# The two local attention stacks as one sequence of 48 rows each, with the feed-forward in pieces between the head pairs

## The reference, cut to what matters

```python
for i in range(DEPTH):                      # DEPTH = 6
    x = attn_layer(shift_tokens(x), Wqkv[i], q_scale[i], k_scale[i], Wo[i]) + x
    x = ffn_layer(shift_tokens(x), ln_g[i], ln_b[i], W1[i], b1[i], W2[i], b2[i]) + x
```

## Time and profile before

| what | us |
|---|---|
| median of 3 runs (lowest, highest) | 6789.9 (6783.46, 6796.57) |
| the profiled execution's own time | 6798.74 |
| its span | 6797.0 |
| TensorE busy | 5769.4 |
| VectorE busy | 4295.0 |
| ScalarE busy | 4171.8 |
| GpSimd busy | 2486.0 |

### The profile page before, as it was taken

How to read it: one execution, slowest core, us unless ns; L and a number is a source line. 1 busy time by engine, 2 the same in 40 slices (tenths; PEclk the granted TensorE clock), 3 DMA queues, 4 the chain that set the end, 5 groups by cost and what they waited for, 6 DMA issues and landing times. The chain is left out here.

```text
span 6797.0 us, 132994 instructions
## 1 busy us (share of the span) xinstructions
PE 5769.4 (85%) x41538; PEld 4249.7 (63%) x41538; DVE 4295.0 (63%) x17058; ACT 4171.8 (61%) x14046; POOL 2486.0 (37%) x2090
## 2 busy tenths in 40 slices
PE   8884798988989898896598898989889898787989
PEld 7773465666656566564366565666656566566778
DVE  4453775767767576774576775757767576444432
ACT  5511675857758586673386775858768586454643
POOL 0000553645445364550354554635455353000000
PEclk9995899999999999997699998999999999888999
DMA  0000000000000000000000000000000000000000
GB/s 10 20 1 2 19 2 18 2 14 5 12 8 2 18 2 15 5 1 3 19 2 14 5 2 18 2 18 2 15 5 2 18 1 2 4 1 3 1 26 7
DMA packets 22465, 54.76 MB, mean 8 GB/s; under 512 B 6728, under 2 KB 16208, under 8 KB 19536
## 3 DMA queue, kind: packets, MB, share of 16 engines
q1 hardware_dynamic: 21712, 45.65, 2.0%
HBM read 44.60 MB, written 1.05 MB: 7 GB/s over the span
## 5 line engine op out<-in xcount | busy, mean ns | idle before, releaser
L1518 PE MATMUL bank<-wA,next_rowT 128*128 128x512 f32 x2304 | 1255.4, 658 | 280.1 <-DVE turnB L1770 199.6
L1615 POOL TENSOR_TENSOR turnA<-raw,ropes 128x512 f32<-128x512 f32 x768 | 969.1, 1272 | 1000.8 <-ACT raw L1665 960.4
L1638 ACT ACTIVATE pairs<-pairs,negmax 128x128 f32<-128x128 f32 (+1 forms) x3072 | 1251.0, 433 | 65.2 <-DVE negmax L1731 63.1
L1731 DVE CUSTOM_DVE_ANT_0 pairs<-bank,bands,rs 128x128 f32<-128x128 f32 (+1 forms) x3072 | 943.5, 363 | 283.2 <-PE bank L1450 263.6
L1622 POOL TENSOR_TENSOR qk<-turnA,turnB 128x512 f32<-128x512 f32 x768 | 969.3, 1272 | 0.0
L1518 PEld LDWEIGHTS bank<-wA,next_rowT 128*128 128x128 f32 x2304 | 389.3, 196 | 774.8 <-DVE turnB L1770 465.6
L1647 ACT ACTIVATE pairsT<-bank 128x256 f32<-128x256 f32 x1536 | 522.5, 407 | 441.1 <-PE bank L1463 441.1
L252 POOL TENSOR_TENSOR rstd<-vareps,neg_half 128x2 f32<-128x2 f32 x152 | 106.2, 699 | 1791.8 <-DVE vareps L241 1791.8
L1638 ACT ACTIVATION_READ_ACCUMULATOR pairs<-pairs,negmax 128x1 f32 x3072 | 669.5, 218 | 0.0
L1628 POOL TENSOR_TENSOR qk<-qk,rs 128x1024 f32<-128x1024 f32 x192 | 365.1, 1902 | 728.5 <-DVE recip L1788 728.5
L1770 DVE TENSOR_TENSOR turnB<-bank,ropes 128x512 f32<-128x512 f32 x768 | 522.4, 680 | 0.0
(11 more groups left out here) (266 smaller groups left out, 11942.1 us busy)
## 6 DMA issues: line engine op xcount, KB each, us to landing
wA<-in_wt_wqkv SPq DMA_DIRECT2D x12, 1536.0 KB, 6.1
wB<-in_wt_wo SPq DMA_DIRECT2D x12, 512.0 KB, 3.2
wC<-in_wt_w SPq DMA_DIRECT2D x12, 341.0 KB, 3.4
wD<-in_wt_w SPq DMA_DIRECT2D x12, 192.0 KB, 3.4
big<-in_e_up SPq DMA_DIRECT2D x1, 2048.0 KB
big<-in_e_down SPq DMA_DIRECT2D x1, 2048.0 KB
scl<-in_wt_scales SPq DMA_DIRECT2D x12, 128.0 KB, 7.4
X<-in_x SPq DMA_DIRECT2D x8, 128.0 KB, 2.3
```

Source lines behind the costliest of these rows:

```text
L1518: pe.matmul(chunk_bank(i)[:, :], c.next_rowT[:, t * P:(t + 1) * P], wqkv[:, k * 512:(k + 1) * 512], start=True, stop=True).then_inc(s.chun ...
L1615: g.tensor_tensor(c.turnA[:, m % 2, :].rearrange("p (h d) -> p h d", h=8), c.raw[:, m % 4, :].rearrange("p (h d) -> p h d", h=8), cos, ALU ...
L1638: last = a.activation(tile, tile, ACT.Exp, scale=-1.0, bias=c.negmax[:, 2 * p + side, t:t + 1], accum_out=c.pair_sums[:, p % 4, t, side:si ...
L1731: last = v.tensor_tensor_reduce(c.pairs[:, 2 * (p % 4) + side, AT[t]:AT[t] + SPAN[t]], c.bank[side][:, AT[t]:AT[t] + SPAN[t]], c.bands[:, ...
```

## The change

A stack becomes one unrolled sequence of 48 windows on every engine, with no loop over layers: window T prepares row T + 1, also where that row is the first of the next layer. The feed-forward of row T - 2 is spread over window T: shift in slot 2, statistics and normalising in slot 3 on VectorE (around the inverse roots, which take two columns more and replace GpSimd's power), transposes of the normalised row in slot 4, the gate products and the gelu in slot 6, the linear products and the hidden product in slot 7. The product back and the addition of row T - 3 stand in slot 1. All of it goes through bank 3, now `ff_bank`; the turned probabilities of both sides share bank 2 and are copied by one instruction. VectorE reads the shifted half where TensorE left it in PSUM, and neither ScalarE nor GpSimd copies it or the row. Each sixth of the projection weights has its own semaphore and is loaded when the last row of the layer before has used it. The last two rows of a stack go through the feed-forward alone (`pe_tail`, `act_tail`, `dve_tail`).

```diff
-PREPARE_IN_FF = {2: ((0,), (1,)), 3: ((2,), ()), 4: ((3,), (4,)), 6: ((5, 6), ()), 7: ((7,), ())}
...
+    ff_bank = c.bank[3]
...
-            probs, out = c.pairs[:, 2 * (p % 4) + side, :], c.bank[2 + side]
+                probs, out = c.pairs[:, 2 * (p % 4) + side, :], c.bank[2][:, S * side:S * side + S]
...
+        def pe_xT(pe, q):
...
+            if has_turn(q - 4):
+                pe.wait_ge(s.hidden_ready, (q - 3) * 3)
+            for t in range(HALVES):
+                last = pe.transpose(ff_bank[:, t * P:(t + 1) * P], c.Y[:, half(q % B, t)], c.ident[:, :])
...
+        def pe_turn_normed(pe, f):
+            pe.wait_ge(s.normed, f + 1)
+            for t in range(HALVES):
+                last = pe.transpose(ff_bank[:, t * P:(t + 1) * P], c.xn[:, t, :], c.ident[:, :])
+            last.then_inc(s.normedT_in_psum, 1)
+        def pe_ff_in(pe, k, side, out):
+            at, n = FF_CHUNKS[k]
+            return pe.matmul(out[0:n, :], w1[:, side * FF + at:side * FF + at + n], c.xT[:, :], start=True, stop=True)
+        def pe_gates(pe, f, bank_free):
+            pe.wait_ge(s.normedT_ready, f + 1)
...
+            pe_ff_in(pe, 0, 1, ff_bank[:, 0:S])
+            pe_ff_in(pe, 1, 1, ff_bank[:, S:2 * S])
+            pe.wait_ge(*bank_free)
+            pe_ff_in(pe, 2, 1, c.bank[7][:, 0:S])
+            pe_ff_in(pe, 2, 0, c.bank[7][:, S:2 * S]).then_inc(s.gates_in_psum, 1)
+        def pe_linear(pe, f):
+            pe.wait_ge(s.gelu_ready, f * 3 + 2)
+            pe_ff_in(pe, 0, 0, ff_bank[:, 0:S])
+            pe_ff_in(pe, 1, 0, ff_bank[:, S:2 * S]).then_inc(s.linear_in_psum, 1)
...
+        def pe_window(pe, T):
+            following = has_turn(T + 1)
+            for p in range(PAIRS):
+                pe_turn_probs(pe, T, p)
...
+                if p == 6 and has_turn(T - 2):
+                    pe_gates(pe, T - 2, (s.qT_copied, (T + 1) * 4 + (1 if following else 0)))
+                if p >= 1:
+                    pe_shares(pe, T, p - 1)
+                    pe_weigh(pe, T, p - 1)
...
+                if p == 1 and has_turn(T - 3):
+                    pe_ff_out(pe, T - 3)
+                if p == 2 and has_turn(T - 2):
+                    pe_shift(pe, T - 2)
+                if p == 4 and has_turn(T - 2):
+                    pe_turn_normed(pe, T - 2)
+                if p == 6 and has_turn(T - 1):
+                    pe_out(pe, T - 1, (s.kT_copied, (T + 1) * 4 + (1 if following else 0)))
+                if p == 7 and has_turn(T - 2):
+                    pe_linear(pe, T - 2)
+                if following:
+                    pe_prepare(pe, T + 1, p, False)
...
-            g.tensor_tensor(c.next_row[:, :, :].rearrange("p t d -> p (t d)"), c.Y[:, row(b)],
-                            c.one[:, 0:1].broadcast_to((P, ROW)), ALU.mult).then_inc(s.row_copied, 1)
...
+        def act_copy_probs(a, T, p):
+            a.wait_ge(s.probsT_in_psum, T * PAIRS + p + 1)
+            a.activation(whole_blocks(c.pairsT[:, 2 * (p % 2):2 * (p % 2) + 2, :]),
+                         c.bank[2][:, :].rearrange("p (n k) -> p n k", n=4), ACT.Identity).then_inc(s.probsT_ready, 1)
...
+                if has_turn(T - 2):
+                    if p == 4:
+                        act_normedT(a, T - 2)
+                    if p == 6:
+                        act_gelu(a, T - 2)
...
-    def act_shifted(a, turn):
...
-        a.activation(c.xn[:, :, hi:D], c.bank[3][:, 0:D].rearrange("p (t d) -> p t d", t=HALVES),
-                     ACT.Identity).then_inc(s.shifted_ready, 1)
...
+        def ff_halves(f):
+            kept = c.Y[:, row(f % B)].rearrange("p (t d) -> p t d", t=HALVES)
+            shifted = ff_bank[:, 0:D].rearrange("p (t d) -> p t d", t=HALVES)
+            return [(t, n, src[:, t, :]) for n, src in enumerate((kept[:, :, 0:D // 2], shifted)) for t in range(HALVES)]
+        def dve_ff_stats(v, f):
...
+            for t, n, src in ff_halves(f):
+                last = v.bn_stats(ff_stats[:, t, n, :], src)
+            step.after(last, v)
...
+        def dve_prepare(v, q, slot, f=None):
...
+                    dve_ff_stats(v, f)
+                    dve_roots(v, ss[:, 0:32 + HALVES], rs[q % 2][:, 0:32 + HALVES])
+                v.memset(c.recip[:, 0, 31:32], 0.0).then_inc(s.rs_ready, 1)
+                if f is not None:
+                    dve_ff_normalise(v, f, rs[q % 2][:, ff_var])
+            if slot == 7:
+                dve_copy_k(v, q, 1)
...
+                if p == 7 and has_turn(T - 2):
+                    dve_last_hidden(v, T - 2)
...
+                if p == 1 and has_turn(T - 3):
+                    dve_ff_add(v, T - 3)
+                ff = T - 2 if p == 3 and has_turn(T - 2) else None
+                if following:
+                    dve_prepare(v, T + 1, p, ff)
...
+                if p == 7:
+                    if has_turn(T - 2):
+                        dve_first_hidden(v, T - 2)
...
+                    for k in WEIGHT_ORDER:
...
+                            sp.wait_ge(s.chunk_in_psum, (T - 1) * N_CHUNKS + CHUNK_ORDER.index((1, k)) + 1)
+                        sp.dma_start(wqkv[:, k * 512:(k + 1) * 512],
+                                     w["wqkv"][d][:, k * 512:(k + 1) * 512]).then_inc(wqkv_loaded[k], 16)
...
+                for T in range(T0, T1):
+                    pe_window(pe, T)
+                pe_tail(pe)
```

More of the change, by code:

```diff
@@ L1350 @@
 N_CHUNKS = len(CHUNK_ORDER)
+WEIGHT_ORDER = (2, 0, 4, 3, 1, 5)
 PE_CHUNK_SLOTS = {j: (2 * j, 2 * j + 1) for j in range(6)}
@@ L1455, in pe_turn_probs @@
-    def pe_turn_probs(pe, turn, p, first):
-        pe.wait_ge(s.probs_ready, turn * PAIRS + p + 1)
-        if not (first and p == 0):
-            pe.wait_ge(s.probsT_ready, turn * PAIRS + p)
-        for side in range(2):
-            probs, out = c.pairs[:, 2 * (p % 4) + side, :], c.bank[2 + side]
-            pe.transpose(out[:, 0:P], probs[:, 0:P], c.ident[:, :])
-            last = pe.transpose(out[:, P:2 * P], probs[:, P + WINDOW:2 * P + WINDOW], c.ident[:, :])
-        last.then_inc(s.probsT_in_psum, 1)
@@ L1548, in pe_prepare @@
-    def pe_prepare(pe, q, slot, alone, first):
-        if slot == 0 and alone:
-            pe_xT(pe, q, True)
-        pe_chunks(pe, q, slot, alone)
-        for i in PE_QKT_SLOTS.get(slot, ()):
-            pe_turn_qk(pe, q, i, first)
-    def pe_out(pe, turn, j):
-        pe.wait_ge(s.ctx_ready, (turn + 1) * PAIRS)
-        for t in range(HALVES):
-            for k in range(8):
-                done = pe.matmul(c.bank[7][:, t * D:(t + 1) * D], ctxT[j][:, k, t * P:(t + 1) * P],
-                                 wo[:, k * D:(k + 1) * D], start=(k == 0), stop=(k == 7))
-        done.then_inc(s.out_in_psum, 1)
@@ L1974, in prepare @@
-                def prepare(turn, slots, weights):
-                    for slot in slots:
-                        if slot == 0:
-                            pe.wait_ge(s.attn_weights, weights)
-                        pe_prepare(pe, turn, slot, True, True)
-                prepare(layer0 * B, range(PAIRS), (layer0 + 1) * n_attn)
-                with pe.Fori(layer0, layer1 - 1) as d:
-                    layer(d, False)
-                layer(layer1 - 1, True)
+                pe_xT(pe, T0)
+                for slot in range(PAIRS):
+                    pe_prepare(pe, T0, slot, True)
@@ L2033, in _ @@
-                prepare(layer0 * B, range(PAIRS))
-                with a.Fori(layer0, layer1 - 1) as d:
-                    layer(d, False)
-                layer(layer1 - 1, True)
+                a.activation(c.cols[:, 30:31], c.neg_half[:, 0:1], ACT.Exp)
+                act_xT(a, T0)
+                for i in range(N_CHUNKS):
+                    act_copy_chunk(a, T0, i)
+                act_copy_q(a, T0, 0)
+                act_copy_q(a, T0, 1)
+                act_probs(a, T0, 0, 0)
+                act_probs(a, T0, 0, 1)
@@ L2082, in _ @@
-                step = dve_steps(v, layer0 * B)
-                prepare(layer0, step, range(PAIRS))
-                step.end()
-                with v.Fori(layer0, layer1 - 1) as d:
-                    layer(d, False)
-                layer(layer1 - 1, True)
+                dve_tables(v, T0)
+                for slot in range(PAIRS):
+                    for m in DVE_ROTATE_SLOTS.get(slot, ()):
+                        dve_rotate(v, T0, m)
+                    dve_prepare(v, T0, slot)
+                    if slot == 6:
+                        dve_copy_k(v, T0, 0)
```

977 lines of the change are left out of this document (471 added, 506 removed).

## The result

The changed kernel takes 6879.16 us (median of 4 runs, 6874.72 to 6881.08) against 6786.68 for the kernel before on the same chip: ratio 1.0134 with a 95% interval of 1.0117 to 1.0152. It is slower by 1.3%, where 6672 us had been predicted. The profiled execution took 6877.37 us. The time is that of rival (d); the experiments have to say whether its mechanism is right too.

What follows compares the result with a forecast made beforehand. A TensorE queue with one VectorE detour bounds the window; 40.98 + 4.83 + 2.05 + 0.15 + 0.3 = 48.3, with 0.7 for the clock 49.0; stacks 297.2 + 4410 = 4707, 118 less, so 6672 us, range 6540 to 6850.

Steps and rivals of the forecast that it cites:

- rival (d): Slot 4's wait lowers TensorE's clock in every window, 3.0 to 3.4 us each; W = 51.3, 6879 us; chance 0.17.
- low clock: Slot 4's longer wait halves TensorE's clock in half of the windows, 1.37 us a fall, 0.7 us on average.
- VectorE's part: Slots 3 and 4: statistics 1.28 and normalising 0.77 lengthen TensorE's open wait by 2.05 us; slot 0 adds 0.15.
- TensorE's part: Feed-forward matmuls add 1.43, 0.7, 1.75 and 0.95 us in slots 1, 2, 6 and 7, all paid, 4.83.
- ScalarE's part: Two table loads a window: the Gelu load free in slot 6, the Exp load in slot 7 costing 0.3 us.
- Rival (c): A table switch costs 1.4 us more than its load on slot 7's chain; W = 50.4, 6798 us; chance 0.08.
- Outside the windows: First windows and ends of the two stacks cost 307.2 us, less 5 us a stack saved at the head.
- Break-even: The window length at which the changed kernel equals the kernel before: W = 50.3 us.
- W: Length of a window with a feed-forward in it, 45 a stack; forecast 49.0 us, 48.3 at full clock.
- The shifted half from PSUM: VectorE reading the shifted half from PSUM was given no surcharge, 0 to 0.2 us.

Runs made afterwards that it cites:

- e4: Changed kernel with six unused 128x256 products filling TensorE's wait ahead of slot 4's transposes; 6828.4 us, ratio 1.0048 to the kernel before.
- e1: Changed kernel with VectorE issuing the four normalisations before the memset that releases GpSimd's scaling of the keys; 6710.07 us, ratio 0.987 to the kernel before.
- e5: Changed kernel with the new orders of e1 and e3 together; 6564.58 us, ratio 0.9667 to the kernel before.
- e12: Changed kernel without the feed-forward row's statistics and normalisation in the windows, transposes running on a constant; 6432.52 us, ratio 0.9466 to the kernel before.
- e11: Changed kernel with Exp in place of the three Gelus, so no table is switched in the windows; 6880.62 us, ratio 1.0129 to the kernel before.
- e2: Changed kernel with the kept half brought to PSUM by two identity products in slot 2, all normalisations reading PSUM; 6785.34 us, ratio 0.9985 to the kernel before.
- e3: Changed kernel with the statistics run ahead of slot 3's last maxima instead of behind them; 6800.86 us, ratio 1.0005 to the kernel before.
- e8: Changed kernel with ScalarE copying the shifted half to SBUF and VectorE reading that copy; 7086.0 us, ratio 1.0432 to the kernel before.
- e13: Changed kernel with the two kept halves normalised by scalar_tensor_tensor in place of tensor_scalar; 6878.83 us, ratio 1.0129 to the kernel before.
- e9: Changed kernel with early statistics, kept half through PSUM, normalisation behind slot 5's last maxima, transposes in slot 6, gate products behind slot 6's weighing; 6481.68 us, ratio 0.9543.

## Why the prediction was wrong

**The sum's terms.** The windows at full clock split slot 4's growth of 5.16 us: 10.69 in the changed kernel, 9.26 with the clock kept (e4), 7.69 without the hold (e1), 6.53 with the statistics moved away (e5), 5.71 without the normalisations (e12), 5.53 before.

| term of slot 4 | predicted us | measured us |
|---|---|---|
| statistics | 1.28 | 7.69 - 6.53 = 1.16 |
| normalisation | 0.77 | 6.53 - 5.71 = 0.82 |
| transposes | 0, inside the wait | 5.71 - 5.53 = 0.18 |
| hold by GpSimd | not there | 9.26 - 7.69 = 1.57 |
| low clock | 0.7 (1.37 in half of the windows) | 10.69 - 9.26 = 1.43 |

The step that failed is "VectorE's part": it priced the normalisations by rows in which GpSimd did nothing (0.61 for two), and never asked what GpSimd does at this point. It does something by the kernel's own order: the memset that stands between roots and normalisations releases its longest instruction. Without the hold and at full clock the window is 48.23 (e1), and the prediction's sum was 48.3. The hold is the 1.57 that lengthened TensorE's wait. The second term that was mis-sized is the clock's, by how often it falls and not by what a fall costs: a fall had been priced at 1.37 us and costs 1.43 in this slot, but it had been taken for half of the windows and comes in all 88, and in 78 of 88 even without the hold (e1). That part alone would have kept the time inside the forecast's range (6540 to 6850): e1, with the clock falling and no hold, takes 6710. The forecast's 6681 for the profiled execution plus 90 x (51.19 - 49.0) = 197 is 6878, and 6877.4 was measured.

**Was it rival (d)?** Its number and place were right, and so was what it said of the clock: the clock is low in slot 4 of all 88 steady windows, which are 50.95 to 51.35 us long, and it is not back for a second stretch in 68 of them, where it stays at half for 6.8 us (3.4 in the other 20). Its price was not: it gave the clock 3.0 to 3.4 us a window, and the clock takes 1.43. Much of the low stretch lies on time in which TensorE waits anyway (0.79 us before 1344.19 and the 1.29 after the transposes), and the windows with 6.8 us are only 0.3 longer than those with 3.4. The rest of its 51.3 was the hold, of which it says nothing, so that its 6879 came out is luck. With the clock kept full (e4) slot 4 is still 9.26. By that rival's mechanism alone e1, which leaves TensorE's queue and VectorE's instructions as they are, could not have gained 1.9 us a window.

**TensorE's part** was right: 1.43, 0.7, 1.75 and 0.95 predicted in slots 1, 2, 6 and 7, and 1.34, 0.67, 1.93 and 1.06 measured, 5.00 in all for 4.83. **ScalarE's part**: the two loads are free (e11), so the 0.3 for the second is 0; slot 0 grew by 0.01 and not by 0.15. Rival (c) falls with e11: with no switch at all the time is the same. **Outside the windows**: the stacks now run from 724.67 to 3181.56 and from 3392.99 to 5850.78 us, together 4914.7; less 90 x 51.19 that leaves 307.6 for their first and last windows, for which 307.2 had been worked out. Their heads are 6.3 and 5.8 us shorter, for 5 each: the first stack begins at 724.67 instead of 730.94, the second 211.4 us behind the first's end instead of 217.2. **Break-even** at W = 50.3 is borne out by e2 and e3: with windows of 50.09 and 50.36 us in the mean their times are 0.9985 and 1.0005 of the kernel before.

**The shifted half from PSUM** had been given nothing, 0 to 0.2, as a cost. As a cost that is right (0.33 against 0.31 us). As a gain it was missed: it is worth 207 us to this kernel (e8).

**What the hold is.** The Trainium skill (SBUF — State Buffer, Who interferes with whom) says that VectorE and GpSimd share one pair of SBUF ports, that they contend for it when VectorE's instruction has two SBUF inputs, or copies or applies scalars from SBUF to SBUF in a mode with two ports, and that "Whoever issues first gets the shared pair for the whole instruction". This case agrees on VectorE's side: a tensor_scalar from SBUF is held until GpSimd's instruction ends (1.90, e8: 1.90, 1.3, 1.3), one that started first is not (0.31), a scalar_tensor_tensor with two SBUF inputs is held (1.94, e13), a reduction of one SBUF input is not (0.69), and a tensor_scalar from PSUM is not (0.33). The reciprocal (0.16, at 1344.06) and the transpose in blocks (0.24, at 1344.56), which read SBUF beside GpSimd, are not held either. No instruction of that kind was tried in place of the normalisation. That GpSimd is held in its turn doesn't show: its scaling starts while the first normalisation still runs and takes 1.91 us, as it does in slot 6 beside none (1.90). That it is the ports which hold VectorE is the Trainium skill's account; the runs show the hold, and which operands and orders bring it.

The warning stood in the trace of the kernel before, in the very instruction by whose row the normalisation had been priced (L245). Of the 192 in the stacks 10 take 1.28 us, each started 0.06 us after an addition on GpSimd:

```profile
L245 DVE TENSOR_SCALAR xn<-xn,mv,rstd x192: 332/344/1287, 1050.4 to 5764.1; 128x128 f32<-128x128 f32 x192
```

This gives the shortest, the median and the longest in ns. The first root step, too, takes 0.17 us at the median, and 0.74 to 1.26 in the 11 of 192 that start beside GpSimd. Here it takes 1.22, until GpSimd's second addition (1118.50 + 2.49) ends, VectorE first and then GpSimd:

```profile
1119.81 1.22 DVE L1786 TENSOR_SCALAR ss<-ss 128x32 f32<-128x32 f32 x1
1121.06 0.18 DVE L704 TENSOR_SCALAR ints<-ss 128x32 int32<-128x32 int32 x1
```

```profile
1118.50 2.49 POOL L1622 TENSOR_TENSOR qk<-turnA,turnB 128x512 f32<-128x512 f32 x2
```

## What to carry to other kernels

Before VectorE work on SBUF operands is put behind an instruction that releases GpSimd, look at what is released: finish the work first and release then (169 us here), or read from PSUM. When pricing an operation by a row, check that the other engines do in that row what they will do at the new place; a maximum far above the median of the same instruction is the sign that they matter. A piece of work that hides by its length alone still costs when it stands ahead of what the bound engine waits for: the same normalisation, not held, cost 0.8 us in slot 4, 1.0 in slot 5 and 0.2 behind slot 5's last maxima, where VectorE was idle and TensorE needed nothing else of it.

## What the runs showed of the hardware

- VectorE's hold is exact and whole: in the changed kernel all 90 normalisations from SBUF that start beside GpSimd's scaling end 0.05 us after it (0.04 for the root steps, 0.08 for L245 before), whatever their own length (0.31, or 0.28 in e13), and in e8 the next two are held by GpSimd's next two instructions. None of the 180 from PSUM beside GpSimd took over 0.34.
- TensorE's clock fell to half after a wait of 1.55 us in 40 of 88 windows of e5 and not in the others, with TensorE doing the same before it in both. In the changed kernel, with waits of 2.76 and 1.29 to 1.54, it fell in every window. With 0.82 (e12) and 1.04 (e9) it never did. What decides it at 1.55 was not found. A window with a fall of 3.4 us was longer than one without by 1.20 us in e1, 1.41 in e4 and 1.42 in e5.
- A switch between Exp and Gelu, 1.28 us twice in a window, was free in a kernel in which ScalarE is busy for 37.5 of 51.3 us.
